# The front of a graph layer in three blocks: norm first, lookups in bf16 beside the product, a segment maximum by edge lane

## The reference

```python
xn = layernorm(x)                       # (x - m) / sqrt(v + 1e-5)
h = xn @ W.T                            # 6250 x 512
e = (h @ a_src)[src] + (h @ a_dst)[dst] # one number an edge, loops added
e = where(e > 0, e, 0.2 * e)
m = segment_max(e, dst)                 # largest of each node's incoming edges
alpha = exp(e - m[dst]); alpha = alpha / segment_sum(alpha, dst)[dst]
gnn = xn + elu(segment_sum(alpha * h[src], dst) + bias)
mix = linear_attention(xn @ Wqkv.T) @ Wproj.T + bproj
x = x + gnn + mix
x = x + mixture_of_experts(layernorm(x))   # 8 experts, the two best of each node
```

## Time and profile before

| | us |
|---|---|
| median of 3 runs | 4465.39 |
| lowest and highest run | 4462.83, 4474.2 |
| profiled execution, its own time | 4469.66 |
| span of that execution, first to last instruction | 4467.9 |
| mean granted TensorE clock | 0.847 |
| busy in the span: PE / DVE / ACT / POOL | 3297.3 / 2373.8 / 1297.3 / 1768.2 |

### The profile page before, as it was taken

One profiled execution on the slowest core, in us unless ns is written; L12 is line 12 of the kernel. 1 busy time (PEld: TensorE's weight loads), 2 busy tenths in 40 slices (PEclk: granted clock), 3 DMA queues, 4 the chain that ended last, 5 costly groups with the idle time before them and its releaser, 6 DMA issues. The chain is left out here.

```text
span 4467.9 us, 74456 instructions
## 1 busy us (share of the span) xinstructions
PE 3297.3 (74%) x11832; PEld 1901.1 (43%) x11833; DVE 2373.8 (53%) x6284; ACT 1297.3 (29%) x3555; POOL 1768.2 (40%) x1993
## 2 busy tenths in 40 slices
PE   4777799999999002777777878888887689999700
PEld 2333699866666001222333333333333355555400
DVE  2333466555555444444555555555556557777733
ACT  0111244311111001544454444444445112222100
POOL 1222344200000001666565555555555136666554
PEclk9888655699999556999998999999999679999955
DMA  3222222366666565665565656555555512222277
GB/s 137 92 93 93 73 77 77 93 155 149 148 142 146 130 133 118 183 184 176 167 191 167 183 164 179 173 176 175 170 182 172 198 43 92 92 92 92 89 233 227
DMA packets 379008, 631.60 MB, mean 141 GB/s; under 512 B 43319, under 2 KB 219610, under 8 KB 377699
## 3 DMA queue, kind: packets, MB, share of 16 engines
q0 software_dynamic: 93472, 318.59, 23.6%
q1 hardware_dynamic: 271395, 287.00, 23.3%
q10 hardware_dynamic: 14112, 25.70, 1.5%
HBM read 538.06 MB, written 93.06 MB: 141 GB/s over the span
## 5 line engine op out<-in xcount | busy, mean ns | idle before, releaser
L975 PE MATMUL acc_ps<-rows,W 128*128 128x512 f32 x1908 | 1041.5, 674 | 348.3 <-DVE W L1079 221.3
L858 POOL DMA_INDIRECT rows<-h_rows,idx x954 | 955.0, 1001 | 737.2 <-PE acc_ps L975 468.9
L975 PEld LDWEIGHTS acc_ps<-rows,W 128*128 128x128 f32 x1908 | 360.1, 209 | 1003.6 <-issue 837.8
L899 ACT ACTIVATE e_pos<-pqb,es_col 128x128 f32<-128x128 f32 x954 | 372.7, 391 | 148.2 <-DVE e_top L1073 131.7
L641 DVE SCALAR_TENSOR_TENSOR masked<-pair,cst 128x192 f32<-128x192 f32 x636 | 250.1, 416 | 309.0 <-DMA pair<-pair_rows 241.4
L1073 DVE TENSOR_TENSOR e_top<-e_pos,e_neg 128x384 f32<-128x384 f32 x318 | 169.8, 558 | 420.0 <-ACT e_neg L900 343.0
L900 ACT ACTIVATE e_neg<-pqb,es_col 128x128 f32<-128x128 f32 x954 | 367.8, 386 | 0.0
L553 PE MATMUL row_ps<-es_lut,hot 49*128 49x128 f32 x1632 | 348.5, 418 | 18.9 <-POOL hot L543 18.9
L553 PEld LDWEIGHTS row_ps<-es_lut,hot 49*128 49x128 f32 x1632 | 348.2, 330 | 19.1 <-issue 19.1
L847 POOL MEMSET zb<- 1x512 bf16 x1 | 0.5, 515 | 890.1 <-POOLq L741 890.1
L1079 DVE SCALAR_TENSOR_TENSOR W<-window,dst_col,e_top 128x128 f32<-128x128 f32 x954 | 275.8, 346 | 60.3 <-PE acc_ps L975 59.3
(11 more groups left out here) (255 smaller groups left out, 4883.8 us busy)
## 6 DMA issues: line engine op xcount, KB each, us to landing
pair<-pair_rows SPq DMA_DIRECT2D x636, 192.0 KB, 4.2
y_rows<-y SPq DMA_DIRECT2D x105, 256.0 KB, 2.0
hi_row<-src_hi SPq DMA_DIRECT2D x204, 128.0 KB, 2.8
rows<-h_rows,idx POOLq DMA_INDIRECT x954, 3.8
xb<-in_x SPq DMA_DIRECT2D x49, 256.0 KB, 2.7
h_rows<-hb ACTq DMA_DIRECT2D x49, 256.0 KB, 2.1
res_rows<-xrest SPq DMA_DIRECT2D x49, 256.0 KB, 2.2
a_own<-h_rows SPq DMA_DIRECT2D x49, 256.0 KB, 2.7
```

Of the source, the lines that this page charges most:

```text
L858: nc.gpsimd.indirect_dma_start(G[j][:], None, h_rows, bass.IndirectOffsetOnAxis(ap=idx[:, j:j + 1], axis=0)).then_inc(row_in[j], 16)
L899: nc.scalar.activation(e_pos[:, half, j, :], pqb[s][:, 0, :], ACT.Exp, bias=es_col[:, ds(at_tile + (half * HT + j), 1)])
L975: nc.tensor.matmul(acc_ps[s][:], W[:, j, :], G[j][:], start=False, stop=False, skip_group_check=True).then_inc(row_used, 1)
```

## The change

The front now has three blocks, and the maximum is arranged anew.

- **Setup.** `wproj` is not loaded here. The source's low part goes to DRAM in bf16 (`src_lo`), its high part stays as `hi_col`. No `pair_rows`.
- **Norm block.** Only layer norm, transposes, the copies to `qT` and the two scores of a node (now copied by ScalarE into `es_n`, `ed_n`), with four buffers of each. VectorE keeps per node 1 + 1/s and -m/s in `ln_keep`.
- **Lookup block.** 102 chunks of 8 edge tiles. The one-hot is now over the 128 low parts and in bf16; the scores are split into three bf16 parts (`es_part`) whose products TensorE sums, 8 x 3 matmuls of 49 columns a chunk. GpSimd makes the even chunks' one-hots, ScalarE the odd ones'. VectorE makes a mask of the high part, multiplies and sums (six operations of 8 x 49 a round). In the first 49 rounds the product h = xn W of one tile stands between the two chunks, with its bias and its store, which SP issues. The all-reduce of the minimum runs at the start of this block. The end puts score less minimum in `hi_col` and its negative in `es_neg`.
- **Maximum block.** `top` is now 128 lanes x 6 edge tiles x 128 nodes. A lane of an edge tile has one edge: VectorE puts its score at its node's column (`masked`, four of six edge tiles); ScalarE does the other two as Relu(score - score x |node - dst|), two operations each. VectorE takes the maximum of `top` and `masked`, half a visit at a time. After a tile, six edge tiles are folded to one (`by_node`); after all tiles, TensorE transposes the 49 and VectorE reduces the lanes. K, V and Q stay as they were. GpSimd clears `top` and makes the residual, for which x is loaded again.
- **Fold.** `wproj` is loaded at its start, by SP; TensorE waits for it. `es2_col` is made here.

```diff
-                                         (wqkv[:], a["wqkv"]), (wproj[:], a["wproj"]), (avec[:], a["avec"]),
+                                         (wqkv[:], a["wqkv"]), (avec[:], a["avec"]),
...
-                        step.done(nc.vector.tensor_copy(lin_d[:], lin_i[:]))
...
-                        step.done(nc.vector.tensor_scalar(lin_i[:], lin_i[:], 7, None, ALU.arith_shift_right))
+                        step.done(nc.vector.tensor_scalar(lin_i[:], lin_i[:], P - 1, None, ALU.bitwise_and))
...
+                        def _(pe):
+                            pe.sem_inc(e_kept, XR)
+                            for now, back in lagged(pe, NT, 1, 1, XR):
+                                if now:
+                                    t, s, i = now
+                                    pe.wait_ge(xn_ready, t + 1 + XR)
+                                    pe.wait_ge(xnT_ready, t + 1)
+                                    for c in range(KC):
+                                        last = nc.tensor.transpose(T_ps[s][:, c * P:(c + 1) * P], xn[s][:, c * P:(c + 1) * P], C["ident"])
+                                    last.then_inc(T_done, 1)
+                                if back:
+                                    t, s, i = back
+                                    pe.wait_ge(xnT_ready, t + 1 + XR)
+                                    pe.wait_ge(e_kept, t + 1)
+                                    for c in range(KC):
+                                        last = nc.tensor.matmul(e_ps[s][:, 0:2], hT[s % 2][:, c, :], u[:, c, :], start=(c == 0), stop=(c == KC - 1))
+                                    last.then_inc(e_done, 1)
...
+                        for j, s, i, has_node in rounds(pool):
+                            if not isinstance(j, int) or j > 0:
+                                pool.wait_ge(rows_done, 2 * j - 1 + 2)
+                            hold(pool, lo_in[2 * s], 16 * i + 16)
+                            nc.gpsimd.tensor_scalar(hot[0][:], lo_row[2 * s][:], C["iota_col"], None, ALU.is_equal).then_inc(hot_ready, 1)
...
+                        for j, s, i, has_node in rounds(act):
+                            act.wait_ge(rows_done, 2 * j + 2)
+                            act.wait_ge(lo_in[2 * s + 1], 16 * i + 16)
+                            nc.scalar.activation(hot[1][:], lo_row[2 * s + 1][:], ACT.Abs, bias=C["minus_col"]).then_inc(apart, 1)
+                            if not isinstance(j, int) or j < NT - 1:
+                                fetch(j + 1, 1 - s)
+                            act.wait_ge(apart, j + 1)
+                            nc.scalar.activation(hot[1][:], hot[1][:], ACT.Relu, bias=C["ones"], scale=-1.0).then_inc(hot_odd, 1)
...
+                            for j in range(LT):
+                                for k in range(3):
+                                    last = nc.tensor.matmul(row_ps[b][:, j * NT:(j + 1) * NT], hot[b][:, j * P:(j + 1) * P], es_part[:, k, :],
+                                                            start=(k == 0), stop=(k == 2))
+                            last.then_inc(rows_done, 1)
+
+                        for j, s, i, has_node in rounds(pe):
+                            lookup(2 * j, 0, hot_ready, j + 1)
+                            if has_node:
+                                pe.wait_ge(fetched, j + 1)
+                                pe.wait_ge(hb_ready, j + 1)
+                                for c in range(KC):
+                                    last = nc.tensor.matmul(h_ps[s][:], hT[s][:, c, :], wg[:, c, :], start=(c == 0), stop=(c == KC - 1))
+                                last.then_inc(h_done, 1)
+                            lookup(2 * j + 1, 1, hot_odd, j + 1)
...
+                        for j, s, i, has_node in rounds(dve):
+                            masks(2 * j, 0)
+                            masks(2 * j + 1, 1)
+                            picks(2 * j, 0)
+                            if has_node:
+                                dve.wait_ge(h_done, j + 3)
+                                dve.wait_ge(h_out[s], 16 * i + 16)
+                                nc.vector.tensor_tensor(hb[s][:], h_ps[s][:], gbias[:], ALU.add).then_inc(hb_ready, 1)
+                            sums(2 * j, 0)
+                            picks(2 * j + 1, 1)
+                            sums(2 * j + 1, 1)
...
+                            with dve.Fori(first, limit, VT) as at_tile:
+                                v = dve.snap((((at_tile + shift) & 0xFFFF) * VISIT) >> 16)
+                                for h in (0, 1):
+                                    hold(dve, topped, 2 * v + h + 1)
+                                    for j in range(h * HT, h * HT + HT - 1):
+                                        put = nc.vector.tensor_scalar(masked[:, j, :], window[:], dst_col[:, ds(at_tile + j, 1)], hi_col[:, ds(at_tile + j, 1)],
+                                                                       ALU.is_equal, ALU.mult)
+                                    put.then_inc(half_ready, 1)
+                                for h in (0, 1):
+                                    hold(dve, half_ready, 2 * v + h + 1)
+                                    hold(dve, act_half, 2 * v + h + 1)
+                                    nc.vector.tensor_tensor(top[s][:, low_half(h), :], top[s][:, low_half(h), :], masked[:, low_half(h), :], ALU.max).then_inc(topped, 1)
+                            last = dve.snap((((limit + shift - 1) & 0xFFFF) * VISIT) >> 16)
+                            hold(dve, topped, 2 * last + 4)
+                            nc.vector.tensor_tensor(folded[:], top[s][:, 0:HT, :], top[s][:, HT:VT, :], ALU.max).then_inc(fold_step, 1)
...
+                                for h in (0, 1):
+                                    j = h * HT + HT - 1
+                                    hold(act, topped, 2 * v + h + 1)
+                                    nc.scalar.activation(masked[:, j, :], window[:], ACT.Abs, bias=dst_col[:, ds(at_tile + j, 1)], scale=-1.0).then_inc(act_apart, 1)
+                                for h in (0, 1):
+                                    j = h * HT + HT - 1
+                                    hold(act, act_apart, 2 * v + h + 1)
+                                    nc.scalar.activation(masked[:, j, :], masked[:, j, :], ACT.Relu, bias=hi_col[:, ds(at_tile + j, 1)],
+                                                         scale=es_neg[:, ds(at_tile + j, 1)]).then_inc(act_half, 1)
...
                             nc.scalar.activation(qT[:, :, ds(t * P, P)], q_ps[:].rearrange("p (c k) -> p c k", c=KC), ACT.Relu).then_inc(q_ready, 1)
+                            masks(t)
...
+                        sp.dma_start(wproj[:], a["wproj"]).then_inc(wproj_in, 16)
```

577 lines of the change are left out of this document (292 added, 285 removed).

## The result

The changed kernel took 3865.23 us (median of 4 runs, 3858.61 to 3867.31), the kernel before it 4465.02 on the same chip (4462.83 to 4474.2): a ratio of 0.8651, 95% interval 0.8635 to 0.8667. The forecast was 4123 with a range from 3975. The gain was 600 us where 342 were forecast, so the direction was right and the size was not. The profiled execution took 3858.61 us around a span of 3856.6.

The account below looks back on a forecast made before the run. TensorE was to bound norm and lookup, TensorE or VectorE each maximum tile. 46.6 + 145 + 20.5 + 447 + 2.5 + 730 + 22.3 = 1413.9 replaces 1756.4 before the aggregation: gain 342.5, forecast 4123 us, range 3975 to 4330.

Parts of the forecast that it names:

- Rounds, 447 forecast: Lookup block: 49 rounds of two chunks and one product at 8.9 us, plus the ends, 447 us.
- the price of a bf16 pair: Lookup chunks: weight load plus 49-column matmul, 0.148 us at half clock, 0.075 at full.
- a floor of 0.055: Lookup chunks: lowest price of a bf16 pair, in us at full clock, with the matmul hidden.
- such a load, twice as fast: Lookup chunks: skill's statement that 128 weights of a type other than FP32 load about twice as fast.
- the 0.6 for handing over: Lookup round: 0.6 us for handing over, beside two chunks and the product, in 7.65 us at full clock.
- the clock: Lookup rounds: mean clock 0.86 as in projection, making 7.65 us a round 8.9.
- full clock throughout: Rival, norm block and lookup chunks: small records run at 2.4 GHz, 110 us less, 3981 us; chance 0.13.
- Norm block, 145 forecast: Norm block: TensorE bounds at 2.75 us a tile with waits, 135 us, plus 10 for filling, draining and end.
- Start of the lookup: Lookup block before its first lookup: TensorE idle behind the all-reduce and a longer one-hot, 20.5 us.
- Maximum block, 730 forecast: Maximum block: each tile the longer of TensorE's 12.25 and VectorE's 4.3 + 2.45 n, with extras 730 us.
- shared access: Maximum block: VectorE slowed beside GpSimd, some 1.5 us in each tile of three visits or more, 25 us.
- the hand-over rival: Rival, maximum block: VectorE and ScalarE pass visits without overlap, 4.0 us each, 160 more, 4283 us; chance 0.13.

Follow-up runs that it names:

- the fourth batch: Batch holding six masks on VectorE and the lagging kernel; slower as a whole, the kernel before took 4730.1 us in it.
- six masks on VectorE: Changed kernel with VectorE building all six masked tiles of a visit and ScalarE none; 3845.89 us, later 3841.26, and ratio 0.8739 in the fourth batch.
- The lagging kernel: Changed kernel with ScalarE building its two masks only in tiles 4 to 23, four tiles late, VectorE all six elsewhere; ratio 0.8716.
- the split: Changed kernel with ScalarE building its two masks only in tiles 0 to 23, VectorE all six in tiles 24 to 48; 3862.04 us.

## Why the prediction was wrong

The sign, the order of the stages and the bounding engine of each were right; the error is one large term and several small ones, nearly all of the same direction.

**Rounds, 447 forecast, about 247 measured.** Two steps failed. First the price of a bf16 pair: "I halve the load for half the bytes, 0.107, and put 0.041 for the matmul on top", 0.075 at full clock, with a floor of 0.055. Measured 0.026 to 0.029, half the floor. The f32 rows of before could not show it, because the load of a full set of 16-bit weights is a case of its own, as 127 columns against 128 show, and I had added load and matmul where they overlap (in the lookup block the loads are busy for 72.1 us and the matmuls for 75.3, side by side). With 127 columns a pair was 0.059 by pitch (2.81 / 48), above the floor and below the 0.075. The prediction had such a load, twice as fast, beside its sum, and gave it no term and no bound. That is 48 x 0.049 = 2.3 us a round, and with the 0.6 for handing over, which did not appear, 2.9: 142 us over 49 rounds. Second the clock: "light ones are some 4.2. I take 0.86". With the pair at a third of its price the light stretch is 1.2 us and not 4.2, and the clock stayed at 2.4 GHz: 7.65 / 0.86 less 7.65 is 1.25 a round, 61 us. The second error may be a child of the first, but that is not shown: with 2.8 us of light work (127 columns) the clock read 1.00 too, with about 16 (f32) 0.67 in the mean, and no run had the 4.2 of the forecast. The rival "full clock throughout" named the right state for the rounds, not for the norm block, and priced it at 6.65 a round, for it kept the floor of the pair.

**The range.** Its lower end, 3975, came from that rival with its floor. I had called 0.055 a floor although no row had such a pair; "the matmul hidden" bounded only the way of overlapping, not the load. An honest lower end would have let the pairs and the handing over cost nothing: a round of 3.5, 49 x 5.4 + 2 x 3.9 = 272 us less than forecast, 3851. The result lies just above it: the rounds took off 200 of these 272, and the other stages, which that end leaves as forecast, nearly 60 more.

**Norm block, 145 forecast, 127.6 measured.** TensorE bounds it and its records have the durations of 1.2 GHz, as forecast. A tile took 2.45 us and not 2.75; the 0.2 of waits per tile was not there, and the two groups of records overlap by 0.1.

**Start of the lookup**, 17.5 against 20.5: right in kind, GpSimd comes to its first one-hot 7.2 us after the all-reduce instead of 11.6.

**Maximum block, 730 forecast, 691.7 measured.** By its steps: VectorE's long tiles fit 4.8 + 2.2 n, where the forecast had 4.3 + 2.45 n and a charge of 25 us for shared access. The visits were too dear by 0.25 x 69 = 17 us over the eleven tiles of four visits and more. Shared access cost about the 0.5 a tile by which 4.8 exceeds 4.3 (the 48 windows beside GpSimd's addition took 0.871 in the mean instead of 0.286), some 6 us in those tiles, since TensorE's 12.2 covers it in most others: 19 less. Three tiles of three visits took 11.4 and not 12.25, the tail 13.4 and not 14. Together these are about 39 for the 38 that were missed. Two slips of the working are small: its terms of a tile add up to 4.4 and not 4.3, and the hand-over rival counts 75 visits in long tiles where its own list has 69. "Hand-over bound" was refuted: a visit stayed at 2.19. My sum took 12.25 or 4.3 + 2.45 n, whichever is longer, tile by tile. That is right for the changed kernel, but I did not ask what makes it so: it is ScalarE's share, which the forecast carried only as a delay of the first mask, and which as a whole is a small loss (some 15 us).

**Fold** and **rest**: 22.1 for 22.3, and 2699.9 for 2711.5; the aggregation, costed as it was, took 1702.8 us in the changed kernel's profile and 1715.5 in the profile before (from the first to the last tile's opening matmul).

## What to carry to other kernels

Price a weight load by its type and by whether it fills all columns; here one column fewer doubled the price of a pair, and f32 in place of bf16 made a record over five times dearer, the lower clock included, and there are two records to a product. Here light work of 1.2 to 2.8 us between dense products ran at the products' clock, and 125 us of small records alone did not: there an added product was cheaper than none. Look which instruction a slow one overlaps in the timeline before moving the neighbour that seems likely. Before an engine takes over a share of another's work, ask which chains its program order ties together; paying the longer of two chains in every tile (618 us here) can cost more than the longer of their sums (600), even where the tiles of one chain got shorter.

## What was not expected of the hardware

In the fourth batch the front ran at the same pace as elsewhere (with six masks on VectorE the lookup's first and last start at 192.2 and 436.2 us, a K, V and Q tile in 12.2), but its aggregation took 2002.7 us at a clock of 0.87, where others took 1699 to 1716 at 0.93 to 0.95:

```profile
1133.00:3135.60 2002.60, 1438.66 (x3587) 591.62 (x3586) 916.01 (x2213) 830.37 (x2684) 967.88 (x1038) 0.87 0.50 151
```

```profile
1157.20:2860.10 1702.90, 1368.93 (x3589) 561.38 (x3588) 909.48 (x2213) 821.96 (x2676) 980.37 (x1038) 0.94 0.59 178
```

The first row is of six masks on VectorE in that batch, the second of the changed kernel in the last one. The lagging kernel beside the first took 1962.4. Both batches carry the same chip number, seven minutes apart, and in the last one the kernel before took 4451.08 us as usual: so it was not a lasting trait of the chip. What it was stays open.

At usual speed the aggregation, which no edit touched, took 1702.5 to 1702.8 us in the three profiles of the changed kernel, 1712.0 with the split, but 1705.7 and 1713.0 in two profiles of one and the same kernel, six masks on VectorE, and 1715.5 in the kernel before. Each figure is of one execution, so these profiles do not show that what the front gains is given back later.
